# Who sums the second modulation's four pieces: TensorE or VectorE

## The reference, cut to what matters

```python
x = data                                            # [2048, 1024]
mod = (silu(c) @ wmod).reshape(1, 6, 1, -1)         # c [1, 1024], wmod [1024, 6*1024]
sa, ca, ga, sb, cb, gb = (mod[:, i] for i in range(6))
ga = (2 * (ga >= 0) - 1) * maximum(abs(ga), 0.25)   # gb likewise
h = layernorm(x) * (1 + ca) + sa
x = x + ga * (h @ masked(weight).T + bias)          # mask: blocks of 32x32
h = layernorm(x) * (1 + cb) + sb
x = x + gb * ffn(h)                                 # gate, up, silu, down; 2752 wide
```

## Time and profile before

| what | value |
|---|---|
| median of 3 runs | 1110.01 us (1108.84 to 1110.47) |
| the profiled execution, its own time | 1110.46 us |
| span of the profiled execution | 1108.7 us |
| TensorE busy | 1080.1 us, 97% of the span |
| VectorE busy | 739.0 us, 67% |
| ScalarE busy | 428.1 us, 39% |
| GpSimd busy | 376.4 us, 34% |

### The profile page before, as it was taken

How to read it: one execution, slowest core, us unless ns; L and a number is a source line. 1 busy time by engine, 2 the same in 40 slices (tenths; PEclk the granted TensorE clock), 3 DMA queues, 4 the chain that set the end, 5 groups by cost and what they waited for, 6 DMA issues and landing times. The chain is left out here.

```text
span 1108.7 us, 13305 instructions
## 1 busy us (share of the span) xinstructions
PE 1080.1 (97%) x4753; PEld 501.3 (45%) x4753; DVE 739.0 (67%) x939; ACT 428.1 (39%) x783; POOL 376.4 (34%) x348
## 2 busy tenths in 40 slices
PE   5999999999999999999999999999999999999998
PEld 3443444545444444444444444444444444444444
DVE  4448478766688998889797888879545434334434
ACT  2322157556564554446555555555432000000000
POOL 2115446647644442326455555655200000000000
PEclk9999999999999999999999999999999999999999
DMA  9994223235453655445666666665298666566430
GB/s 345 388 388 114 80 72 95 68 103 162 143 194 129 169 174 171 129 125 166 195 205 180 184 191 184 186 203 180 74 353 330 246 251 235 223 240 235 194 127 38
DMA packets 132049, 206.94 MB, mean 187 GB/s; under 512 B 20624, under 2 KB 99216, under 8 KB 129552
## 3 DMA queue, kind: packets, MB, share of 16 engines
q1 hardware_dynamic: 126688, 184.08, 50.4%
q0 software_dynamic: 5296, 22.02, 5.6%
HBM read 137.39 MB, written 68.68 MB: 186 GB/s over the span
## 5 line engine op out<-in xcount | busy, mean ns | idle before, releaser
L1436 PE MATMUL pA<-work 128*128 128x512 f16 x1680 | 377.0, 379 | 5.1 <-ACT work L1097 3.3
L1436 PEld LDWEIGHTS pA<-work 128*128 128x128 f16 x1680 | 163.8, 98 | 205.4 <-ACT work L1097 6.4
L1236 PE MATMUL pA<-work 128*128 128x512 f32 x512 | 227.3, 595 | 2.5 <-DVE work L1696 0.9
L1436 PE MATMUL pB<-work 128*128 128x512 f16 x752 | 175.9, 379 | 1.4 <-DVE work L1855 1.4
L1236 PEld LDWEIGHTS pA<-work 128*128 128x128 f32 x512 | 94.3, 190 | 112.9 <-issue 109.9
L1877 DVE SCALAR_TENSOR_TENSOR work<-work 128x512 f16<-128x512 f16 x144 | 122.7, 874 | 19.6 <-ACT work L1117 19.3
L1503 PE MATMUL pA<-work 128*128 128x512 f16 x600 | 134.4, 379 | 0.0
L1097 ACT ACTIVATE work<-pA 128x512 f32<-128x512 f32 x126 | 74.6, 592 | 116.3 <-PE pA L1436 111.0
L1436 PEld LDWEIGHTS pB<-work 128*128 128x128 f16 x752 | 73.5, 98 | 90.2 <-DVE work L1855 2.1
L946 ACT ACTIVATE work<-pB,small 128x128 f32<-128x128 f32 x240 | 86.8, 478 | 70.6 <-PE pB L1209 59.3
L1503 PE MATMUL pB<-work 128*128 128x512 f16 x480 | 107.5, 379 | 0.9 <-DMA work<-h_left_scratch 0.9
(11 more groups left out here) (178 smaller groups left out, 1058.9 us busy)
## 6 DMA issues: line engine op xcount, KB each, us to landing
work<-h_scratch SPq DMA_DIRECT2D x8, 4480.0 KB, 13.7
h_scratch<-work SPq DMA_DIRECT2D x60, 512.0 KB, 3.1
work<-in_L_wmod SPq DMA_DIRECT2D x10, 2048.0 KB, 16.6
work<-in_L_ffn_gate_w SPq DMA_DIRECT2D x84, 128.0 KB, 3.2
work<-in_L_ffn_up_w SPq DMA_DIRECT2D x84, 128.0 KB, 2.9
work<-down_scratch SPq DMA_DIRECT2D x7, 1280.0 KB, 11.5
work<-in_L_ffn_down_w SPq DMA_DIRECT2D x68, 128.0 KB, 2.8
work<-in_L_attn_data SPq DMA_DIRECT2D x16, 512.0 KB, 4.2
```

Source lines behind the costliest of these rows:

```text
L1236: last = pe.matmul(pA[:, 2 * par(t) + h, :], hT1[par(t)][:, c, :], wT[:, c, h * H:(h + 1) * H], start=(c == 0), stop=(c == KT - 1))
L1436: last = pe.matmul(ps, w[:, m, c], bc[b][:, mv_, s, c], start=begin, stop=(i == n - 1 and c == KT // 2 - 1 and s == 1), skip_group_check=True)
```

## The change

Pieces 6 to 9 (rows 3 and 4) are no longer summed by TensorE: `row_sum(6)` to `row_sum(9)` and ScalarE's `copy_row(6)` to `copy_row(9)` go. VectorE sums them itself with the new `sum_piece`: one `tensor_scalar` and seven chained `scalar_tensor_tensor` of 128x512 f32 a piece, straight into `acc[v]`. The sum over partitions is left to `columns`, with a weight of 1 in place of 1/32. `row_sum(4)`, `row_sum(5)` and `gate_row(2)` move ahead by half a tile's product, so that the gate row comes directly behind `attend(1, 1)`. `transpose(1, 0)` goes from t = 3 to t = 4. VectorE's hand-written order is new: the gating of tiles 0 and 1 (`scale_evacuated`) comes ahead of both additions; a `sum_piece` stands ahead of `gate_a`, behind `normalise(1, 0)`, behind `residual(3)` and behind `residual(4)`.

```diff
-        MID = {3: 0, 6: 1, 7: 3, 8: 5, 9: 6, **{t: t - 2 for t in range(10, NT + 1)}}
+        MID = {4: 0, 6: 1, 7: 3, 8: 5, 9: 6, **{t: t - 2 for t in range(10, NT + 1)}}
...
-                    sp.wait_ge(row_summed, 9)
+                    sp.wait_ge(piece_summed, 4)
...
+                if n:
+                    pool.wait_ge(rstd_done[L], n)
...
             copy_row(4)
+            copy_row(5)
             evacuate(1)
-            copy_row(5)
...
-                if t == 2:
-                    for m in range(6, 10):
-                        copy_row(m)
...
             def columns(v, dst):
-                pe.wait_ge(row_copied, 2 * v + 2)
+                if v in SUMMED_BY_DVE:
+                    pe.wait_ge(piece_summed, 2 * SUMMED_BY_DVE.index(v) + 2)
+                else:
+                    pe.wait_ge(row_copied, 2 * v + 2)
...
+            row_sum(4)
             attend(1, 1, range(4, 6))
-            row_sum(4)
+            row_sum(5)
             attend(1, 1, range(6, KT))
-            row_sum(5)
+            gate_row(2, rowp[0])
...
-                if t == 2:
-                    attend(t, 0, range(4))
-                    gate_row(2, rowp[0])
-                    attend(t, 0, range(4, KT))
-                elif t <= LAST:
+                if t <= LAST:
                     attend(t, 0)
...
                     pe.wait_ge(ga_ready, 1)
-                    row_sum(6)
-                    row_sum(7)
-                if t == 3:
-                    pe.wait_ge(row_copied, 10)
+                if t == 4:
+                    pe.wait_ge(row_copied, 6)
...
-                if t == 2:
-                    for m in (8, 9):
-                        pe.wait_ge(row_copied, m - 1)
-                        row_sum(m)
...
+            def sum_piece(m):
+                v, h = m // 2, m % 2
+                dst, w = acc[v][:, H * h:H * (h + 1)], mp[m].rearrange("p (t n) -> p t n", t=KT)
+                dve.wait_ge(piece_loaded[m], 16)
+                if v == 3:
+                    dve.wait_ge(w_turned, 12)
+                else:
+                    dve.wait_ge(acc_used, 3)
+                dve.wait_ge(silu_c_done, 1)
+                link(dve.tensor_scalar(dst, w[:, 0], csil[:, 0:1], None, ALU.mult))
+                for t in range(1, KT):
+                    step = dve.scalar_tensor_tensor(out=dst, in0=w[:, t], scalar=csil[:, t:t + 1], in1=dst,
+                                                    op0=ALU.mult, op1=ALU.add)
+                    if t < KT - 1:
+                        link(step)
+                step.then_inc(piece_summed, 1)
...
             normalise(0, 3)
+            sum_piece(6)
             gate_a()
-            residual_of_evacuated(0)
+            scale_evacuated(0)
+            scale_evacuated(1)
+            finish(0)
+            finish(1)
+            stats1(4)
+            normalise(0, 4)
+            residual(2)
             normalise(1, 0)
-            residual_of_evacuated(1)
-            stats1(4)
+            sum_piece(7)
+            stats1(5)
+            normalise(0, 5)
+            residual(3)
+            sum_piece(8)
             dve.wait_ge(scales_loaded, 16 * 2 * (A + 1))
             bound_of(2, sgs)
             bound_of(3, sus)
-            normalise(0, 4)
-            residual(2)
-            stats1(5)
-            normalise(0, 5)
-            normalise(1, 1)
-            residual(3)
             stats1(6)
             normalise(0, 6)
+            normalise(1, 1)
             residual(4)
+            sum_piece(9)
             cols2()
```

More of the change, by code:

```diff
@@ L297, in adaln_kernel @@
         row_copied = sem("row_copied")
+        piece_summed = sem("piece_summed")
         evacuated = sem("evacuated")
@@ L383, in adaln_kernel @@
         last_stored = sem("last_stored")
+        SUMMED_BY_DVE = (3, 4)
         SUM_ORDER = [0, 2, 1, 3, 4, 5, 6, 7, 8, 9]
@@ L1253, in columns @@
             def columns(v, dst):
-                pe.wait_ge(row_copied, 2 * v + 2)
+                if v in SUMMED_BY_DVE:
+                    pe.wait_ge(piece_summed, 2 * SUMMED_BY_DVE.index(v) + 2)
+                else:
+                    pe.wait_ge(row_copied, 2 * v + 2)
+                weight_ = one if v in SUMMED_BY_DVE else share
                 for a in range(A):
-                    last = pe.matmul(dst[Q * a:Q * (a + 1)], share.to_broadcast([P, Q]), acc[v][:, 2 * P * a:2 * P * (a + 1)],
+                    last = pe.matmul(dst[Q * a:Q * (a + 1)], weight_.to_broadcast([P, Q]), acc[v][:, 2 * P * a:2 * P * (a + 1)],
                                      start=True, stop=True)
@@ L1640, in residual, with scale_evacuated @@
                 finish(t)
-            def residual_of_evacuated(t):
+            def sum_piece(m):
[14 more added lines that the diff above has]
+                step.then_inc(piece_summed, 1)
+            def scale_evacuated(t):
                 dve.wait_ge(evacuated, t + 1)
                 link(dve.tensor_tensor(x1[t], x1[t], ga, ALU.mult))
-                finish(t)
             def turn_unit(u):
@@ L1842, in _ @@
                     normalise(0, t + 2)
-                if t in MID and t > 3 and t <= LAST:
+                if t in MID and t > 4 and t <= LAST:
                     normalise(1, MID[t] + 1)
```

## The result

| | before | changed |
|---|---|---|
| median, 4 runs each | 1109.74 us | 1124.32 us (1123.97 to 1124.40) |
| ratio, 95% interval | | 1.0128 [1.0115, 1.0141] |
| profiled execution, own time | 1110.46 us | 1124.40 us |
| span | 1108.7 us | 1122.3 us |

The change makes the kernel 14.6 us slower. The direction was forecast, with 9.6 us; 1124.3 lies 1.8 us above the range. The two profiled executions differ by 13.94 us, 13.6 of them in the span.

What follows compares the result with a forecast made beforehand. TensorE, busy 97%, was taken to set the end; the last VectorE sum would hold its columns until 146.9 instead of 137.26 us, so 1110.0 + 9.6 = 1119.6 us, range 1112.5 to 1122.5.

Steps and rivals of the forecast that it cites:

- The chain on VectorE: VectorE's ordered work from piece 6 to the last sum, with waits: columns ready at 146.9 us against 137.26.
- rival E: GpSimd's two tiny instructions also block a step of pieces 7 to 9: 2.2 us more, 1121.8 us; 8%.
- B: GpSimd's addition waits for the end of a VectorE piece, so pieces cost 6.0 us: +6.8, 1116.8 us; 11%.
- C: Not slower: GpSimd's additions hold VectorE up nowhere; columns at 136.45 us, -0.8, 1109.2 us; 8%.
- D: The change saves what TensorE's rows offer, 8.4 us: 1101.6 us; 6% with a partial form at 1105.
- F: A chained step of VectorE's sums costs only its columns, 0.52 us: 5.5 us less, 1114.1 us; 5%.
- The step that failed: Behind line 1256's columns, everything was taken to shift by their delay, 9.6 us, through to the end.
- a wait behind the columns that was there before: Sign that the forecast is wrong: such a wait takes in part of the 9.6 us shift.

Runs made afterwards that it cites:

- e11: The changed kernel with GpSimd's add_bias for tiles 4, 5 and 6 made to wait until VectorE's current piece is summed: 1121.48 us.
- e4: The changed kernel with the sums of pieces 8 and 9 back on TensorE, in its wait ahead of transpose(0, 4): 1107.79 us.
- e9: e4 with GpSimd's add_bias(2) put ahead of its two tiny instructions rstd_of(1, 0): 1105.33 us.
- e2: The kernel before with 47 idle products on TensorE right ahead of the columns, a pure delay: 1121.17 us.
- e1: The changed kernel with 19 and 44 idle products on TensorE in its waits ahead of transpose(0, 4) and the columns' second half: 1122.15 us.
- e7: The kernel before with 32 chained one-column instructions added on VectorE in its wait for the gate row: 1110.91 us.
- e3: The changed kernel with the sum of piece 7 moved ahead of stats1(4), into VectorE's wait for x(4): 1121.69 us.
- e8: The changed kernel with 24 more chained one-column instructions on VectorE in its wait for x(4): 1122.95 us.
- e10: The changed kernel run once more, unchanged, beside the kernel before: 1124.30 us.
- e6: e4 with finish(0) put back ahead of the second scaling, as in the kernel before: 1107.59 us.

## Why the prediction was right in kind and short in size

**The chain on VectorE held, to the last sum.** Gate ready 80.95 forecast, 80.95 measured; first `finish` 88.8 and 88.78; `normalise(0, 4)` 100.55 and 101.23; `normalise(0, 5)` 116.6 and 117.02; `normalise(0, 6)` 132.75 and 132.99; last sum's end 146.35 and 146.39. A piece was put at 6.0 alone and 8.05 beside an addition, and took 6.01 and 7.95. Where it ran late, by 0.6 us at x(4), a tiny instruction of GpSimd was at work, one step earlier than rival E had it and the other way round: VectorE's addition held up the one ahead of `add_bias(2)`, which took 1.06 us instead of 0.19.

**Of the rivals**, B (an addition waits for the whole piece) is refuted: GpSimd's additions began within the pieces, at the price forecast. C (no exclusion) is refuted by e11. E (the tiny instructions lengthen pieces 7 to 9) would have made a piece 8.8 us long; in e11 they still fall into piece 8, and its seven steps take 5.48. D asked for sums hidden in VectorE's idle time; e4 and e9 show it for two of them. F is refuted: seven steps took 5.48 us, 0.78 each.

**The step that failed** is the one after the columns: "what follows hangs on these columns in both kernels, so I let the shift of 146.9 - 137.26 = 9.6 us run through to the end". e2 shows that a shift does run through, so the mechanism stands. But the term was too small, for two reasons.

First, the prediction had TensorE standing for some 4 and 13 us and gave its work behind the waits the old durations: 0.5 for half the columns, the old timeline after them. At 1.2 GHz the half of the columns took 1.0 (so that the transposes began at 147.46 instead of 146.9), the transposes 0.83 more and the products 0.76. In the same way the two half products behind the first wait took 14.98 instead of 13.74, which ate the 1.5 us of waiting forecast ahead of `transpose(0, 5)` and cost nothing more. e1 gives these 2 us back.

Second, the change of stage was taken as unmoved, and costs 1.8 us. The prediction named "a wait behind the columns that was there before", but only as something that could shorten the shift. Of the 1.8, the 1.3 us of waiting for VectorE recur, as 0.9 to 1.34, in each profile of kernels with four sums on VectorE; the other 0.5, a longer wait for a load, lies within what that wait differs by among the other kernels (0.92 to 1.91, and 4.11 in e7). The sum is 9.6 + 0.6 at the columns + 1.6 of clock + 1.8 = 13.6; the rest to 14.6 is 0.3 outside the span and 0.7 by which the profiled execution before was slower than its median.

**What stays open** is why the load of x1 at the change of stage lands later. All six profiles of kernels in which VectorE sums four pieces show TensorE waiting for VectorE there, 0.9 to 1.34 us (the changed kernel, e1, e3, e8, e10, e11); of the others none does. A later start (e2) doesn't bring it, and a longer list on VectorE (e7) doesn't either. The stretches of the changed kernel just ahead of it, and those of the kernel before at the same distance from the loads' issue, show when the bytes move, not why:

```profile
869.65:871.65 2.00, 0.89 (x5) 0.20 (x2) 1.21 (x2) 0.00 (x0) 0.00 (x0) 1.00 0.96 300
871.65:873.65 2.00, 1.77 (x9) 0.85 (x10) 0.08 (x1) 0.00 (x0) 0.00 (x0) 1.00 0.07 21
```

```profile
858.00:860.00 2.00, 2.00 (x11) 0.88 (x9) 0.00 (x0) 0.00 (x0) 0.00 (x0) 1.00 0.99 305
860.00:862.00 2.00, 2.00 (x11) 0.94 (x10) 0.00 (x0) 0.00 (x0) 0.00 (x0) 1.00 0.96 271
```

In the changed kernel, the first of these, the last transfers run at 21 GB/s and 0.07 of the engines' time, about one engine of 16, for nearly 2 us, as if one were behind the rest. But stretches of 2 us hide that the kernel before has such a tail too, ended by SP's next load:

```profile
859.79:860.79 1.00, 1.00 (x6) 0.49 (x5) 0.00 (x0) 0.00 (x0) 0.00 (x0) 1.00 0.07 21
...
860.61 0.33 SPq L670 DMA_DIRECT2D work<-h_scratch  x1
```

There it shows for 1 us only, since SP's next loads go out at 860.61, 15.8 us behind its loads of x1; in the changed kernel they go out 17.4 us behind them, at 873.85. A stretch of 1 us at 0.04 to 0.14 stands there in all thirteen profiles, so the tail alone doesn't set the kernels with four sums apart. That one engine lags, and that x1 waits for it in these kernels only, is argued and not shown.

## What to carry to other kernels

Idle time of an engine is worth only what its order of work leaves of it: four sums of 6 us were moved into 32 us of idle time, and two of them found a place (e4, e9) while the last two, ahead of what TensorE waited for, cost more than the 3.6 us that TensorE had spent on them (16.5 us between the changed kernel and e4). Write the receiving engine's chain out with its waits for loads, for the way over a third engine and for the exclusion at SBUF, and compare its end with the deadline on the giving engine. When the forecast has TensorE standing for several us, price the first work behind the wait at half clock (here 1.6 to 2.3 us lost), and look at where the next burst of loads falls.

## What the runs showed of the hardware

- TensorE's clock fell to 0.50 in waits of 4.85, 8.41 (e3) and 10.11 us, with 1.6 to 2.3 us lost behind the last; it stayed at 1.00 where the waits were about 1 us long (e4, in every stretch of 5 us from 95 to 160 us). The Trainium skill (TensorE: Matmul & The Clock Gate, Part 1) gives the clock these two levels only, and the granted 0.50 agrees.
- One-column instructions of GpSimd, 0.19 and 0.55 us when alone, took 1.05 and 1.54 beside VectorE's scaling and addition (e6), and what hung on the addition behind them came late: the 512 KB of x(4) were there at 98.49 us, and at 95.05 where the addition stood ahead of them (e9).
